# The experts' share of the work, one part begun while tokens are still routed: a transformer layer with routed experts on one NeuronCore

## The reference, cut to what matters

```python
x = x + attention(layernorm(x))        # landmark attention with a 13-tap conv, x is [4, 1024, 256]
y = layernorm(x).reshape(4096, 256)
logits = y @ router_w.T                # 8 experts
weights, selected = sparsemixer_eval(logits, 0.01)     # two experts for each token
for e in range(8):                     # w_gate, w_up: [512, 256], w_down: [256, 512] for each expert
    h = silu(y @ w_gate[e].T) * (y @ w_up[e].T)
    out = out + dense_w[:, e:e+1] * (h @ w_down[e].T)
x = x + out
```

## Time and profile before

| what | value |
|---|---|
| median of 3 runs | 1206.57 us |
| the profiled execution | 1203.91 us |
| its span | 1202.2 us |
| PE busy | 1127.5 us (94%) |
| DVE, ACT, POOL busy | 612.3, 300.8, 303.7 us |
| mean granted TensorE clock | 0.983 |
| gate and up matmuls (L1458) | 267.2 us in 2272 instructions |
| down matmuls (L1468) | 134.5 us in 568 instructions |
| weight copies of the tiles (L1067, DVE) | 91.8 us in 71 |

### The profile page before, as it was taken

How to read it: one execution, slowest core, us unless ns; L and a number is a source line. 1 busy time by engine, 2 the same in 40 slices (tenths; PEclk the granted TensorE clock), 3 DMA queues, 4 the chain that set the end, 5 groups by cost and what they waited for, 6 DMA issues and landing times.

```text
span 1202.2 us, 24795 instructions
## 1 busy us (share of the span) xinstructions
PE 1127.5 (94%) x9834; PEld 912.8 (76%) x9834; DVE 612.3 (51%) x1283; ACT 300.8 (25%) x535; POOL 303.7 (25%) x297
## 2 busy tenths in 40 slices
PE   3999999999988899999999999649999999999997
PEld 3767667676677756677767767549999999999996
DVE  7354342233267466676686677654444444444442
ACT  4432222222233322332333233211111111111110
POOL 5000000000010003235534553524322323224332
PEclk9999999999999999999999999769999999999999
DMA  9300000000110030211322222333232232322321
GB/s 341 122 1 1 1 1 1 1 1 1 54 40 5 3 140 19 103 56 63 134 75 79 68 95 69 112 107 46 48 50 46 47 49 46 50 47 43 48 44 12
DMA packets 48704, 68.19 MB, mean 57 GB/s; under 512 B 8272, under 2 KB 42192, under 8 KB 47568
## 3 DMA queue, kind: packets, MB, share of 16 engines
q1 hardware_dynamic: 34288, 45.92, 12.1%
q0 software_dynamic: 13296, 16.92, 8.2%
q10 hardware_dynamic: 1008, 3.78, 0.8%
HBM read 41.05 MB, written 26.46 MB: 56 GB/s over the span
## 4 chain that ended last, share of the span: by engine, by line
PE 90%; DVE 3%; issue 3%; POOL 1%; ACT 1%; DMA 1%; POOLq 0%; SPq 0%; DVEq 0%; ACTq 0%
PE ps L1458 21%; PE ps L1468 10%; PE ps L1360 10%; PE ps L1158 9%; PE ps L1138 9%; PE ps L1399 9%; PE ps L1391 5%; PE ps L1149 3%; PE ps L1272 2%; PE ps L1379 1%; PE ps L1452 1%; PE ps L1101 1%; PE ps L1345 1%; PE ps L1113 1%; PE ps L1256 1%
## 5 line engine op out<-in xcount | busy, mean ns | idle before, releaser
L1458 PEld LDWEIGHTS ps<-mem 128*128 128x128 f32 x2272 | 266.6, 193 | 4.5 <-DVE mem L1067 0.9
L1458 PE MATMUL ps<-mem 128*128 128x128 f32 x2272 | 267.2, 276 | 0.6 <-ACT mem L697 0.6
L508 POOL DMA_INDIRECT out<-mem x71 | 126.4, 1780 | 278.6 <-DVE mem L1061 201.7
L1468 PE MATMUL ps<-mem 128*128 x568 | 134.5, 380 | 0.9 <-DVE mem L1080 0.9
L463 POOL TENSOR_TENSOR mem<-mem,small 128x1024 f32<-128x1024 f32 x36 | 68.5, 1904 | 248.7 <-DVE small L986 115.6
L1360 PE MATMUL ps<-mem 128*128 128x512 f32 x288 | 129.7, 594 | 1.3 <-DVE mem L870 1.3
L705 ACT ACTIVATE mem<-ps 128x512 f32<-128x512 f32 x71 | 42.4, 598 | 326.4 <-PE ps L1458 326.4
L1399 PE MATMUL ps<-mem 128*128 128x256 f32 x512 | 120.7, 390 | 0.0
L1138 PE MATMUL ps<-mem 128*128 128x512 f32 x256 | 115.4, 593 | 0.0
L1158 PE MATMUL ps<-mem 128*128 128x256 f32 x512 | 113.2, 379 | 0.9 <-DVE mem L762 0.9
L1158 PEld LDWEIGHTS ps<-mem 128*128 128x128 f32 x512 | 97.2, 190 | 20.7 <-issue 7.2
(11 more groups left out here) (198 smaller groups left out, 1286.1 us busy)
## 6 DMA issues: line engine op xcount, KB each, us to landing
mem<-xs_d SPq DMA_DIRECT2D x71, 130.0 KB, 2.1
mem<-w_gu SPq DMA_DIRECT2D x8, 1024.0 KB, 5.8
mem<-x SPq DMA_DIRECT2D x8, 512.0 KB, 7.8
mem<-x SPq DMA_DIRECT2D x32, 128.0 KB, 2.2
out<-mem SPq DMA_DIRECT2D x32, 128.0 KB, 1.7
mem<-w_down SPq DMA_DIRECT2D x8, 512.0 KB, 5.8
xnt_d<-mem ACTq DMA_DIRECT2D x3, 1056.0 KB, 5.7
mem<-xnt_d SPq DMA_DIRECT2D x3, 1056.0 KB, 4.9
```

The lines of the kernel that those rows point to most:

```text
L508: pool.indirect_dma_start(out=out_rows, out_offset=bass.IndirectOffsetOnAxis(ap=xs[:, v, D + 1:D + 2].bitcast(U32), axis=0), in_=ys[:, v], ...
L1458: mm = pe.matmul(bank(2 * c + u)[:, f * P:(f + 1) * P], wgu[:, u, k, c, f * P:(f + 1) * P], xst[:, u, k], start=(k == 0), stop=(k == KD - 1))
L1468: mm = pe.matmul(bank(4 + u)[:, 0:D], hid[:, u, f * P:(f + 1) * P], w_d_s[:, e, f], start=(f == 0), stop=(f == 3))
```

## The change

The expert work is cut in another way, and a part of it is moved to where the last groups are routed.

- **Early rows.** After group 4 (20 tiles of tokens) is placed, DVE picks the expert with most rows so far (`choose_early`, 8 small instructions, in step 31). 5120 rows are placed by then, so it has at least 640. SP loads its gate and up weights (1 MB) to a buffer of their own and its first 640 rows after step 33 (`first_rows`). They are 5 blocks of 128 rows: two units of 256 and one tile of 128.
- **Units.** An item is now a unit (two blocks, 256 rows of one expert) or a tile (one block). After the 3 early items come 22 units, taken from the front of the experts' rows, and then 22 tiles for what is left. 5 + 44 + 22 blocks are 71, as before. A unit is worked off in two steps, each with 256 rows and half of the 512 hidden columns, so that a step has as many columns on each engine as a tile had. One weight copy on DVE serves a unit; its two output blocks are accumulated over both steps in PSUM banks 4 and 6.
- **Two tables.** The table of units needs only the sizes (`sizes`, `table` with 22 entries, signal `d_units`); that of the tiles is computed later (`units_taken`, `table` again, `d_tiles`). Zero rows are written after the first four units are loaded, all by SP.
- **Order.** The last steps of the token loop are written out by hand on PE, ACT and DVE, with the early blocks between the routing of groups 7 and 8. Every item now waits for all additions of the item before it to land (POOL); the five early blocks, all of one expert, don't wait for one another. The ring of rows has 16 blocks. Logits and counts of the last three groups go to other PSUM banks (1, 5, 5).

The diff, cut to its core:

```diff
+EARLY = 4
+EROWS = 2 * P * sum(n for _, n in GROUPS[:EARLY + 1]) // (E * P) * P
+LATER = 2 * TOK - EROWS
+NU = -(-(LATER - E * (2 * P - 1)) // (2 * P))
+NT = (LATER + E * (P - 1)) // P - 2 * NU
+EBLK = EROWS // P
+ITEMS = [2] * (EBLK // 2) + [1] * (EBLK % 2) + [2] * NU + [1] * NT
+NEARLY = EBLK // 2 + EBLK % 2
+STEP_OF = [(a, h) for a, n in enumerate(ITEMS) for h in range(n)]
+NSTEP = len(STEP_OF)
+BLOCK = [sum(ITEMS[:a]) for a in range(len(ITEMS) + 1)]
+FIRST = NEARLY
...
+def down_bank(a, b):
+    return 4 + 2 * (b if ITEMS[a] == 2 else a % 2)
...
+            def first_rows():
+                sp.wait_ge(s("c2_sim"), 3 * CT)
+                sp.wait_ge(s("d_early"), 1)
+                e = sp.value_load(early[0:1, 0:1].bitcast(I32), min_val=0, max_val=E - 1)
+                sp.dma_start(wgu_e, w_gu[bass.ds(e, 1)].rearrange("o k p g f -> p (o k) g f")).then_inc(s("e_w_in"), 16)
+                for u in range(2):
+                    for v in range(G):
+                        sp.wait_ge(s(f"d_sc{u}{v}"), 32 * sent_before(EARLY + 1, u, v))
+                r = sp.value_load(early[0:1, 1:2].bitcast(I32), min_val=0, max_val=(E - 1) * REGION)
+                sp.dma_start(xs_e, xs_d[bass.ds(r, EROWS), :].rearrange("(u p) c -> p u c", p=P)).then_inc(s("e_xs_in"), 16)
...
+            def unit_rows(i):
+                a = FIRST + i
+                v = (BLOCK[a] - EBLK) % XRING
+                slot_free(a)
+                r = sp.value_load(u_row[0:1, i:i + 1].bitcast(I32), min_val=0, max_val=ZROW - 2 * P)
+                sp.dma_start(xs[:, v:v + 2], xs_d[bass.ds(r, 2 * P), :].rearrange("(u p) c -> p u c", p=P))\
+                  .then_inc(s(f"m_unit_in{i % 8}"), 16)
+
...
+            for i in range(4):
+                unit_rows(i)
+            for e in range(E):
+                pad_region(sp, e)
+            for i in range(4, NU):
+                unit_rows(i)
+            sp.wait_ge(s("d_tiles"), 1)
+            sp.wait_ge(s("d_pad_out"), 16 * (E + 1))
+            for i in range(NT):
+                tile_rows(i)
...
+            for r in range(EBLK):
+                wait_alone(pool, "m_y", r + 1)
+                add_rows(r, xs_e[:, r])
+            for a in range(FIRST, len(ITEMS)):
+                for r in range(BLOCK[a - 1] if a > FIRST else 0, BLOCK[a]):
+                    pool.wait_ge(s(f"m_sc{r % YRING}"), 16 * (r // YRING + 1))
+                for r in range(BLOCK[a], BLOCK[a + 1]):
+                    wait_alone(pool, "m_y", r + 1)
+                    add_rows(r, xs[:, (r - EBLK) % XRING])
...
+            norm_columns(NG - 2, 0)
+            gap_exponentials(NG - 3)
+            rows_transposed(0)
+            gap_exponentials(NG - 2)
+            gate_out(0)
+            norm_rows(NG - 1, 0)
+            norm_rows(NG - 1, 1)
+            gate_out(1)
+            norm_columns(NG - 1, 0)
+            rows_transposed(1)
+            gap_exponentials(NG - 1)
+            gate_out(2)
+            gate_out(3)
+            rows_transposed(2)
+            gate_out(4)
+            rows_transposed(3)
...
+            def units_taken():
+
+                ch.link(dve.tensor_scalar(te, te, -1.0, float(NU), ALU.mult, ALU.add))
+                ch.link(dve.scalar_tensor_tensor(out=te, in0=te, scalar=0.0, in1=nt, op0=ALU.max, op1=ALU.min))
+                ch.step(dve.scalar_tensor_tensor(out=base, in0=te, scalar=2.0 * P, in1=base, op0=ALU.mult, op1=ALU.add))
+                ch.link(dve.scalar_tensor_tensor(out=n_e, in0=te, scalar=-2.0 * P, in1=n_e, op0=ALU.mult, op1=ALU.add))
...
+            def hidden_out(n):
+                dve.wait_ge(s("m_sil"), n + 1)
+                dve.wait_ge(s("m_up"), n + 1)
+                if n >= 2:
+                    dve.wait_ge(s("m_down"), n - 1)
+                dve.tensor_tensor(hid[:, n % 2], sil[:, n % 2], bank(2 + n % 2), ALU.mult).then_inc(s("m_hid"), 1)
+
+            def rows_weighed(a):
+                dve.wait_ge(s("m_down"), BLOCK[a + 1])
+                for r in range(BLOCK[a], BLOCK[a + 1]):
+                    rows = xs_e[:, r] if r < EBLK else xs[:, (r - EBLK) % XRING]
+                    if r >= YRING:
+                        dve.wait_ge(s(f"m_sc{r % YRING}"), 16 * (r // YRING))
+                    dve.tensor_scalar(ys[:, r % YRING], bank(down_bank(a, r - BLOCK[a]))[:, 0:D], rows[:, D:D + 1], None, ALU.mult)\
+                       .then_inc(s("m_y"), 1)
+
+            def expert_weights(a):
+                w, n = a - FIRST, a - FIRST - NU
+                source = u_eid[0:1, w:w + 1] if n < 0 else t_eid[0:1, n:n + 1]
+                e = dve.value_load(source.bitcast(I32), min_val=0, max_val=E - 1)
+                if w >= 2:
+                    dve.wait_ge(s("m_up"), BLOCK[a - 1])
+                dve.tensor_copy(wgu[:, w % 2], w_gu_s[:, e]).then_inc(s("m_w"), 1)
+
...
+            hidden_out(0)
+            slots(NG - 2)
+            hidden_out(1)
+            choices(NG - 1)
+            slots(NG - 1)
+            sizes()
+            table(2 * P, 0, 8, NU, u_eid, u_row, "d_units")
+            hidden_out(2)
+            rows_weighed(0)
             dve.wait_ge(s("wgu_in"), 16 * E)
...
+            dve.wait_ge(s("c2_y"), MT)
+            dve.wait_ge(s("d_units"), 1)
+            expert_weights(FIRST)
+            hidden_out(3)
+            units_taken()
+            table(P, P - 1, 7, NT, t_eid, t_row, "d_tiles")
+            expert_weights(FIRST + 1)
+            rows_weighed(1)
+            hidden_out(4)
+            dve.wait_ge(s("d_tiles"), 1)
+            for n in range(BLOCK[FIRST], NSTEP):
+                a, h = STEP_OF[n]
+                if h == 0:
+                    rows_weighed(a - 1)
+                hidden_out(n)
+                if h == ITEMS[a] - 1 and a + 2 < len(ITEMS):
+                    expert_weights(a + 2)
+            rows_weighed(len(ITEMS) - 1)
...
+            def x_columns(a):
+                n = ITEMS[a]
+                rows_in(a)
+                if a >= 1:
+                    pe.wait_ge(s("m_xst"), a)
+                for k in range(KD):
+                    for i in range(n):
+                        r = BLOCK[a] + i
+                        rows = xs_e[:, r] if r < EBLK else xs[:, (r - EBLK) % XRING]
+                        mm = pe.transpose(bank(7)[:, (k * n + i) * P:(k * n + i + 1) * P], rows[:, k * P:(k + 1) * P], idt)
+                mm.then_inc(s("m_xtp"), 1)
+
+            def hidden(c, n):
+                a, h = STEP_OF[n]
+                w = wgu[:, (a - FIRST) % 2] if a >= FIRST else wgu_e
+                if c == 0:
+                    if a >= FIRST:
+                        pe.wait_ge(s("m_w"), a - FIRST + 1)
+                    pe.wait_ge(s("m_xst"), a + 1)
+                    if n >= 2:
+                        pe.wait_ge(s("m_hid"), n - 1)
+                size = ITEMS[a] * P
+                per = 2 * F // size // 2
+                for i in range(per):
+                    f = per * h + i
+                    for k in range(KD):
+                        mm = pe.matmul(bank(2 * c + n % 2)[:, i * size:(i + 1) * size], w[:, k, c, f * P:(f + 1) * P],
+                                       xst[:, a % 2, k, 0:size], start=(k == 0), stop=(k == KD - 1))
+                mm.then_inc(s(("m_gate", "m_up")[c]), 1)
+
...
+            def down(n):
+                (a, h), u = STEP_OF[n], n % 2
+                e = expert(a)
+                pe.wait_ge(s("m_hid"), n + 1)
+                size = ITEMS[a] * P
+                per = F // size
+                before = a - 2 if ITEMS[a] == 1 and ITEMS[a - 2] == 1 else a - 1
+                if h == 0 and before >= 0:
+                    pe.wait_ge(s("m_y"), BLOCK[before + 1])
+                for b in range(ITEMS[a]):
+                    for i in range(per):
+                        f = per * h + i
+                        mm = pe.matmul(bank(down_bank(a, b))[:, 0:D], hid[:, u, i * size + b * P:i * size + (b + 1) * P],
+                                       w_d_s[:, e, f], start=(f == 0), stop=(f == 3))
+                mm.then_inc(s("m_down"), 1)
+
+            for i in range(QT + 2):
+                token_step(i)
+            last = QT + 2
+            c2_tp(NG - 2, 0)
+            pe.wait_ge(s("c2_cvt"), cvt_count(QT - 1))
+            bank6_read(last)
+            c2_lg(NG - 2, 0)
+            c2_counts(NG - 3)
+            x_columns(0)
+            c2_y(MT - 1)
+            pe.wait_ge(s("e_w_in"), 16)
+            pe.wait_ge(s("c2_sub"), QT)
+            hidden(0, 0)
+            hidden(1, 0)
+            c2_counts(NG - 2)
+            pe.wait_ge(s("d_taken"), NG - 2)
+            hidden(0, 1)
+            hidden(1, 1)
+            c2_tp(NG - 1, 0)
             pe.wait_ge(s("wd_in"), 16 * E)
...
+            down(0)
+            pe.wait_ge(s("d_taken"), NG - 1)
+            c2_lg(NG - 1, 0)
+            x_columns(1)
+            down(1)
+            c2_counts(NG - 1)
+            hidden(0, 2)
+            hidden(1, 2)
+            hidden(0, 3)
```

(18 more changed lines are left out.)

291 lines of the change are left out of this document (123 added, 168 removed).

## The result

The changed kernel takes **1188.62 us** (median of 4, 1188.55 to 1189.22), the kernel before in the same comparison 1206.48 (median of 4): ratio 0.9851, 95% interval 0.9839 to 0.9864. That is 17.9 us less; the forecast was 20.8 less, 1185.8 us. The profiled execution of the changed kernel took 1188.56 us, with a span of 1186.8 and a mean granted clock of 0.991.

What follows compares the result with a forecast made beforehand. PE, busy 94% of the span, was taken as the bound. First regular gate matmul 810.0 + slow clock 3.25 + remainder 360.3 = 1173.55 for the last matmul, 20.8 less; forecast median 1185.8 us, 8-in-10 range 1178.5 to 1193.

Steps and rivals of the forecast that it cites:

- The remainder of the stage: First regular gate matmul to last matmul: 395.0 less 27.6 (five blocks), 5.1 (units) and 2.0 (slow clock), 360.3 us.
- The value chosen for 256 columns: Gate and up in units: 216 ns a matmul, saving 0.23 us a unit, 5.1 for 22; bounds 0 and 5.1.
- Units keep PE full: Expert stage: a unit's cycle is 10.81 us, weighings have 2.9 us to spare, so the cost is nothing.
- The token stage and the early steps: PE from 766.8 through last projection, early steps 0 and 1 and down 0, which ends at 780.3.
- The routing chain: Group 8's logits to the sizes on DVE: logits at 781.2, choices 2.88 us, then 2.63; sizes begin at 786.8.
- logits, 0.9: 781.2: Group 8's logits on PE right after down 0: 0.9 us, ending at 781.2, only 0.4 later than before.
- The two table waits: PE stands 3.0 us behind DVE's unit table (790.1 to 793.15) and 2.65 us behind the tile table.
- the two falls: Granted clock drops to 0.50 for 6.5 us behind each table wait, the second stretch costing 3.25 us.
- 1 (the clock stays up): Clock holds in one or both table waits: 1179.5 us with no drop, 1182.5 with the first alone; chance 0.21.
- 2: Units save nothing at 256 columns, or wait 0.2 us each: 5.1 us of gain lost, 1190.9 us; chance 0.15.
- 3: Transition between tokens and experts runs at 1.2 GHz throughout: about 11 us longer, 1197 us; chance 0.07.
- 4: POOL's additions become the bound, deciding from 11.75 us a unit; at 13.8 the kernel is slower, 1252 us; chance 0.03.

Runs made afterwards that it cites:

- e3: Changed kernel with each gate and up matmul of a 256-row item split into two of 128 columns: 1191.01 us.
- e10: Changed kernel without early rows: 25 units, 21 tiles, both tables ahead of the first product: 1202.84 us, ratio 0.9939 to the kernel before.
- e1: Changed kernel with the load of expert 7's gate and up weights issued after the last logits instead of after the last projection: 1187.39 us.
- e4: Changed kernel with POOL's four scatters of group 7 held until group 8 has chosen: 1184.41 us, ratio 0.9814 to the kernel before.
- e6: Changed kernel, unchanged, run again for the spread of its transition: four times 1180.4, 1180.5, 1187.2 and 1189.3 us; profiled execution 1187.23.
- e8: Changed kernel with both DVE's order changed around the two tables and POOL's scatters of group 7 held until group 8 has chosen: 1183.69 us.
- e11: Changed kernel, unchanged, run once more with more rounds; profiled execution 1182.50 us.
- e12: Changed kernel with DVE's order changed around the two tables, repeated with more rounds: 1182.68 us, ratio 0.9774 to the kernel before.
- e9: Changed kernel with POOL's scatters of groups 6 and 7 all held until group 8 has chosen: 1187.67 us.
- e7: Changed kernel with DVE weighing the first item and making step 2's hidden rows before the unit table, tile table later in halves: 1183.51 us.
- e5: The kernel before, unchanged, run again for its trace on this chip: 1207.8 us.
- the nine later runs: Changed kernel, unchanged, run again in two later comparisons: 1180.43 to 1182.50 us (four runs) and 1187.23 to 1189.33 us (five).

## Why the prediction came out

**The remainder of the stage: right.** 359.9 us at full clock against 360.3, with 5 x 5.52 and 22 x 0.23 in it; e3 shows the 0.23 a unit on its own, and e10 the sum of it within 0.1 us once the clock is taken off. The value chosen for 256 columns, from two groups of other lines, was the upper bound of the two, and it held. Units keep PE full, as argued: 10.80 us against 10.81, no gap in 356 us. The Trainium skill's fixed cost of about 2.5 ns a matmul (TensorE: Matmul & The Clock Gate, "Wait — 56ns, not 53.3ns?") would have made a unit of two times 128 columns an estimated 0.08 us longer; e3 measures 0.23, or 7.2 ns for each of the 32 matmuls more. The measurement decides.

**The token stage and the early steps: right, a little late.** Down 0 ends at 784.03 against 780.3 + 1.7 = 782.0. 0.6 of the 2.0 us are there when the counts of group 6 end (769.07 instead of 768.5): PE waits 3.41 us before the logits of group 7, for DVE's residual (L957), since the program has PE wait there until PSUM bank 6 is read. The rest is the half-clock stretch behind this wait, which meets the last projection (4.74 us for 3.46). This wait is already the hold-up of the next paragraph. The logits of group 6 end at 758.93, DVE gets the signal at 762.62, and the residual stands behind the choices that wait for it:

```profile
762.64 0.19 DVE L983 COPY mem<-ps 128x32 f32<-128x32 f32 x1 [2.42 <-remote]
...
765.81 0.42 DVE L957 TENSOR_TENSOR mem<-ps,mem 128x256 f32<-128x256 f32 x1
```

**The routing chain: wrong, by 7.0 us more.** The step "logits, 0.9: 781.2" took each signal of PE as instantly there. Logits ended at 791.93, 9.0 after 781.2 + 1.7 = 782.9. The cause as far as the runs show it: while POOL issues scatters in a row, a busy PE's signals come late. In ten traces (the changed kernel, e1 to e4, e6 to e8, e11, e12) the last of the held-up signals come 1.5 to 2.5 us after the end of the row, wherever it ends between 781.1 and 788.1, and single ones within it; without the row (e9) they are on time. Why the chip does so is open, and so is why the trace shown of before has no late signal.

**The two table waits: the mechanism right, the prices too high.** 1.67 and 2.42 us against 3.0 and 2.65; the unit table took 4.2 us against 4.45. Behind the first the clock did not fall at all, behind the second for 3.4 us instead of 6.5. The forecast charged 6.25 us for the two falls; measured is 1.7 for the second. Together with the shorter waits, and less a stretch of 6.8 us at 0.50 behind the wait before the logits that the forecast did not have, this gave back 5.3 us by the last matmul: 2.0 + 7.0 - 5.3 = 3.7 us late, 1178.99 against 1173.55 + 1.7. e7 shows both waits to be DVE's order: turned round, these two vanish, and two shorter ones come.

**So the forecast of 1185.8 was right partly by luck: two errors partly cancel.** The profiled execution was forecast at 1183.1 and took 1188.56, 5.5 us more: 3.7 of the transition and the 1.7 by which the trace of before was early. At the medians only 2.8 are left, because the forecast added 2.66 us for the distance between that trace and the median of before. e5, at 1207.8, shows what such a distance holds: 1.55 us before the last convolution, and an estimated 1.7 of the hold-up that the trace of before does not have. By the nine later runs the forecast lies in the gap between the kernel's two heaps (1187 to 1189 and 1180 to 1182.5).

**Rivals.** 1 (the clock stays up) was half true, for the first wait only, and its time is that of the lower heap by coincidence of terms. 2 fell with e3. 3 fell: the clock is 1.00 from 772.1 to 789.0, and at 0.50 only for the 6.8 us after that. 4 fell: POOL's additions of a unit are issued 1.86 us apart (908.83, 910.69), the next unit's at 919.63, landing at a median of 3.8 us, as in the earlier trace rows:

```profile
908.83 1.55 POOL L554 DMA_INDIRECT out<-mem  x1 [7.38 <-DVE mem L1130]
910.69 1.56 POOL L554 DMA_INDIRECT out<-mem  x1 [0.30 <-issue]
919.63 1.55 POOL L554 DMA_INDIRECT out<-mem  x1 [7.38 <-DVE mem L1130]
```

(The chain of 13.8 us that this rival named took the longest issues, 2.51 us; at the medians it is 0.85 + 1.56 + 0.3 + 1.56 + 7.6 = 11.9, just past its own bound of 11.75.) Ahead of each unit POOL stands 7.38 us for DVE's weighing. The additions land 3.6 to 5.4 us after their issue (820 to 1050 us), so a landing has about 2 us to spare at the least. Only among the tiles does POOL stand for landings, 16 times and 50.0 us together, as it did in the kernel before (19 times, 59.8).

## What to carry to other kernels

Work that fills one engine's waits can bring that engine into conflict with what another does at the time. Look at what the idle engines (here POOL with its scatters) issue in the microseconds in which the critical chain hangs on signals of a busy TensorE. Moving the row of scatters shortened the wait (e4, e9), but the hold-up moved along (e8, e9), and a gain in time stayed unshown. When a chain of small steps decides between two orders, one profiled execution may show only one of two outcomes; run both kernels often enough to see heaps before 5 us are explained. And on an engine that serves both a bookkeeping chain and the main loop, serve first whoever has someone waiting now: that took 4.2 us out of the transition in the traces of one job (e7 and e6).

## What the runs showed of the hardware that was not expected

- Signals of finished matmuls arrived up to 9 us late (e12: transposes ended at 781.5, signal at 790.6) while POOL issued indirect DMAs back to back and PE was busy. With PE mostly idle in the same row of scatters its waits were 4.86, 0.78 and 3.08 us and none grew to 6 (e10). One execution of the kernel before has no late signal at all, another has some twenty (e5).
- DVE's own steps were mostly not slowed: in the changed kernel its slots of group 7 run from 780.6 to 782.1 at 0.2 us a step, in the midst of the row. But behind the end of the row single steps of DVE waited for the step before them, 0.51 us in e5 (788.31, row ended 786.2) and 0.46 and 0.53 in e10 (789.83 and 790.54, row ended 788.2).
- In the changed kernel the first signals after the start of the row are still on time; the first late one is that of 778.3, after five scatters.
- The granted clock fell to 0.50 (1.2 GHz) for 3.4 us after the table waits of 2.42, 2.57 and 2.69 us (changed kernel, e11, e6), for 6.8 after the wait of 6.06, for 6.8 to 10.2 after those of 7.54 to 8.18 (e1, e6, e7, e12); after table waits of 1.67, 1.93 and 2.30 us it stayed at 1.00 (2.4 GHz). The waits of 2.2 us at 754 were followed by 3.4 us at 0.50 in e6 and by none in the changed kernel and e11, so the length of the wait alone does not decide. Nor did it in the other variants: table waits of 2.10 (e3) and 2.13 us (e4) were followed by 3.4 us at 0.50, a wait of 2.88 us (e8) by none.
- A gate or up instruction in fp32 with 128 columns took 111.6 ns in a row of its like (3.57/32), one with 256 columns 216 (3.45/16).
